# Cross-attention 0 of a four-part model: query weights folded into the keys, output weights into the values

## The reference, cut to what matters

```python
def _attn(x, ctx, Wq, Wk, Wv, Wo, bo):
    q = (x @ Wq).reshape(b, n, HEADS, DHEAD)
    k = (ctx @ Wk).reshape(b, m, HEADS, DHEAD)
    v = (ctx @ Wv).reshape(b, m, HEADS, DHEAD)
    scale = DHEAD ** (-0.5)
    sim = jnp.einsum('bihd,bjhd->bhij', q, k) * scale
    attn = jax.nn.softmax(sim, axis=-1)
    out = jnp.einsum('bhij,bjhd->bihd', attn, v).reshape(b, n, INNER)
    return out @ Wo + bo
...
h = _ln(x, g2, be2)
x = _attn(h, context, Wq2, Wk2, Wv2, Wo2, bo2) + x
```

## Time and profile before

| | us |
|---|---|
| median of 3 runs | 7044.72 |
| lowest, highest | 7041.6, 7048.59 |
| the profiled execution's own time | 7048.18 |
| its span (first to last instruction) | 7046.4 |

### The profile page before, as it was taken

The page is one execution under the profiler, slowest core; times in us unless marked ns, Lnnn a source line. Parts: engine busy times, 40 slices in busy tenths (PEclk is TensorE's granted clock), DMA queues, the critical chain, the costliest instruction groups (busy, mean ns, idle before and its releaser), DMA issues. The chain is left out here.

```text
span 7046.4 us, 74355 instructions
## 1 busy us (share of the span) xinstructions
PE 6239.0 (89%) x20890; PEld 2611.0 (37%) x20890; DVE 5161.7 (73%) x6021; ACT 3737.4 (53%) x6881; POOL 4712.8 (67%) x2193
## 2 busy tenths in 40 slices
PE   9999999999998888888888888888888888888898
PEld 4444445455343233322333222323222333223334
DVE  4444444454223999999999999999999999995623
ACT  4444444322223666666666666666666666664432
POOL 3333333211202999999999999999999999993300
PEclk9999999999999898999999998989898999999998
DMA  2000000100201232333323242323233333332000
GB/s 72 0 0 0 0 0 0 54 9 6 102 0 42 62 86 70 76 90 75 84 67 84 61 100 64 88 59 90 65 96 76 73 82 69 78 83 54 5 0 24
DMA packets 235646, 378.49 MB, mean 54 GB/s; under 512 B 62785, under 2 KB 71681, under 8 KB 233777
## 3 DMA queue, kind: packets, MB, share of 16 engines
q1 hardware_dynamic: 235312, 374.71, 21.9%
HBM read 202.29 MB, written 19.20 MB: 31 GB/s over the span
## 5 line engine op out<-in xcount | busy, mean ns | idle before, releaser
L2428 POOL TENSOR_TENSOR work<-work,weights 128x1024 f32<-128x1024 f32 x1152 | 2691.4, 2361 | 19.4 <-DMA weights<-mamba_bc 13.0
L2287 PE MATMUL banks<-work 128*64 128x512 f32 x4608 | 1371.2, 677 | 599.4 <-POOL work L2433 584.8
L2350 DVE TENSOR_TENSOR_SCAN banks<-banks,work 128x512 f32<-128x512 f32 x1296 | 1616.8, 1270 | 64.3 <-ACT banks L2397 64.3
L2397 ACT ACTIVATE banks<-work 128x512 f32<-128x512 f32 x2304 | 1497.7, 680 | 67.4 <-DVE work L2128 43.2
L2350 DVE TENSOR_TENSOR_SCAN work<-banks,work 128x512 f32<-128x512 f32 x1008 | 1264.4, 1269 | 102.1 <-ACT banks L2397 77.8
L2433 POOL TENSOR_TENSOR work<-work,weights 128x1024 f32<-128x1024 f32 x504 | 1187.4, 2356 | 92.3 <-ACT work L2020 92.3
L1860 PE MATMUL banks<-work,weights 128*128 128x512 f32 (+31 forms) x3796 | 1168.8, 459 | 3.0 <-DVE work L2101 3.0
L570 POOL TENSOR_TENSOR work<-work 128x1024 f32<-128x1024 f32 x256 | 484.0, 1893 | 801.6 <-DVE work L458 801.6
L1860 PEld LDWEIGHTS banks<-work,weights 128*128 128x128 f32 x3796 | 645.5, 193 | 625.2 <-issue 547.3
L2146 DVE TENSOR_TENSOR work<-banks,weights 128x512 f32<-128x512 f32 x1296 | 852.7, 669 | 0.0
L2287 PEld LDWEIGHTS banks<-work 128*64 128x64 f32 x4608 | 266.2, 144 | 1466.7 <-POOL work L2433 884.8
(11 more groups left out here) (297 smaller groups left out, 7641.0 us busy)
## 6 DMA issues: line engine op xcount, KB each, us to landing
weights<-mamba_bc SPq DMA_DIRECT2D x592, 256.0 KB, 5.0
work<-work SPq DMA_DIRECT2D x1160, 128.0 KB, 2.3
weights<-mamba_taps SPq DMA_DIRECT2D x5, 2048.0 KB, 7.3
mamba_taps<-work SPq DMA_DIRECT2D x4, 2048.0 KB, 6.9
work<-in_conv_rows SPq DMA_DIRECT2D x16, 256.0 KB, 6.7
out_T<-X SPq DMA_DIRECT2D x8, 512.0 KB, 3.3
X<-in_xT SPq DMA_DIRECT2D x2, 1536.0 KB, 13.0
weights<-in_in_w SPq DMA_DIRECT2D x5, 512.0 KB, 3.9
```

The lines of the kernel that those rows point to most:

```text
L2287: mm = e.matmul(ybank[k % 2][64 * h:64 * h + 64, :], fold, ring_pair(n, j)[:, h, :], start=False, stop=(a == SP_ - 1))
L2350: e.tensor_tensor_scan(ub if by_pool(j) else da, da, ub, state[:, i:i + 1], ALU.mult, ALU.add).then_inc(scanned, 1)
L2397: e.activation(banks[:, slot_of(i), :], dt_rep[:, k % 2, h, :], ACT.Exp, scale=decay[:, f:f + 1]).then_inc(da_full, 1)
L2428: e.tensor_tensor(ring_pair(n, j), u_rep[:, k % 2], bc[:, a, 0, :].unsqueeze(1).to_broadcast([P, 2, TC]), ALU.mult) \
```

## The change

cross_attention_0 is written anew. Keys are projected as before, values now with features on partitions. Then, for each head, the output weights are multiplied into the values (fold_values, 64 products over 64 partitions) and the query weights into the keys (fold_keys, 32 products over 64 partitions); heads alternate between partitions 0 to 63 and 64 to 127, and each of the pair writes a bank of its own. The folded keys (kq) stay in SBUF in four regions, some of them where weights lay. The folded values of all batches (8 MB) go to DRAM in four parts (lay) and come back one batch at a time (bring). Wq2 is passed in transposed. In the loop over tiles there is no query projection and no mixing: scores are 4 products of 512 columns over the normed features, and the output is 8 products for each of two halves straight from the transposed probabilities. The copy of a turned tile is one ScalarE operation on 1024 columns. The norm's scale is one GpSimd operation, its affine part stands behind the turned copy of tile t = 3.

VectorE's list and the set-up are left out here but for the regions:

```diff
+    folded, at = core.area(at, 3, 8, B * M)
+    keys, _ = core.area(2 * KD * T + KD * T + T, tiles, B * M)
+    values, _ = core.area(2 * KD * T + KD * T + T + QT * heads * M, tiles, B * M)
+    wq, wo = wview(core, side, 0, 8, D), wview(core, side, 6144, 8, D)
+    wk, wv = wview(core, side, 2048, 2, INNER), wview(core, side, 4096, 2, INNER)
+    wide = wview(core, side, 2048, 8, B * M)
+    kq = {(0, 0): folded[:, 0], (0, 1): folded[:, 1], (1, 0): folded[:, 2], (1, 1): wide}
+    REGIONS = ((0, 0), (0, 1), (1, 1), (1, 0))
+    staged = [core.weights[side][:, 2048:6144].rearrange("p (h e) -> p h e", h=heads),
+              folded[:, 2].rearrange("p h n -> p (h n)").rearrange("p (h e) -> p h e", h=heads),
+              wview(core, 0, 0, heads, D), wview(core, 0, 4096, heads, D)]
+    vo = [wview(core, side, 0, chunks, D), wview(core, side, 6144, chunks, D)]
...
+            def lay(p):
+                for half in range(2):
+                    for parity in range(2):
+                        e.wait_ge(copied[parity], (FOLDED_V + 8 * p + 4 * half + 4) // 2)
+                    e.dma_start(vo_dram[p][:, 8 * half:8 * half + 8, :], staged[p][:, 8 * half:8 * half + 8, :]).then_inc(laid[p], 16)
+
+            def bring(b):
+                for h in range(2):
+                    own = slice(width * h, width * h + width)
+                    src = vo_dram[b // 2][b % 2 * M:b % 2 * M + M, :, :].rearrange("m (c t) e -> m t c e", t=2)
+                    e.dma_start(vo[b % 2][own, :, :], src[:, h, :, :]).then_inc(vo_in[b % 2], 16)
+
+            for p in range(B // 2):
+                lay(p)
+            e.wait_ge(laid[0], 32)
+            e.wait_ge(copied[0], MADE // 2)
+            e.wait_ge(copied[1], MADE // 2)
+            bring(0)
+            bring(1)
+            e.wait_ge(laid[1], 32)
+            e.wait_ge(laid[2], 32)
+            e.wait_ge(laid[3], 32)
             load_weights(e, core, 0, [(0, d["L0_xattn_Wp"]), (4096, d["L0_xattn_W2"]), (6144, d["L1_xattn_pre_w1"]), (6656, d["L1_xattn_pre_w2"])])
             for b in range(2, B):
+                v_lane_read(e, ("out0", b - 2))
+                s_lane_read(e, ("out1", b - 2))
+                bring(b)
...
+            def bank_free(i):
+                if i >= RING_B:
+                    e.wait_ge(copied[i % 2], (i - RING_B) // 2 + 1)
+
+            def project_context(at):
+                for i in (at, at + 1):
+                    bank_free(i)
+                for k, r in enumerate(CROWS):
+                    for i in (at, at + 1):
+                        w, j = (wk, i) if i < VALUES else (wv, i - VALUES)
+                        mm = e.matmul(bank_of(i), w[0:r, k, j * P:(j + 1) * P], core.C[0:r, k, :], start=(k == 0), stop=(k == 1))
+                        if k == 1:
+                            mm.then_inc(made, 1)
+
+            def fold_values(at):
+                p, w = divmod(at - FOLDED_V, 8)
+                for i in (at, at + 1):
+                    bank_free(i)
+                for s in range(4):
+                    h, i = 2 * w + s, at + s % 2
+                    mm = e.matmul(bank_of(i)[:, s // 2 * D:s // 2 * D + D], values[rows_of(h), h // 2, p * P:(p + 1) * P], wo[rows_of(h), h // 2, :],
+                                  start=True, stop=True)
+                    if s >= 2:
+                        mm.then_inc(made, 1)
+
+            def fold_keys(at):
+                r, first = divmod(at - FOLDED_K, 8)
+                k, half = REGIONS[r]
+                for i in (at, at + 1):
+                    bank_free(i)
+                for s in range(2):
+                    h = 8 * half + first + s
+                    e.matmul(bank_of(at + s), wq[rows_of(h), h // 2, k * P:(k + 1) * P], keys[rows_of(h), h // 2, :], start=True, stop=True) \
+                        .then_inc(made, 1)
+
+            def project_out(b):
+                e.wait_ge(t_free, (b + 1) * QT)
+                e.wait_ge(vo_in[b % 2], 32 * (b // 2 + 1))
+                v_lane_free(e, ("out0", b))
+                for c in range(chunks):
+                    mm = e.matmul(lane_v, vo[b % 2][:, c, 0:P], probsT[:, c, :], start=(c == 0), stop=(c == chunks - 1))
+                mm.then_inc(ln.v_full, 1)
+                s_lane_free(e, ("out1", b))
+                for c in range(chunks):
+                    mm = e.matmul(lane_s, vo[b % 2][:, c, P:D], probsT[:, c, :], start=(c == 0), stop=(c == chunks - 1))
+                mm.then_inc(ln.s_full, 1)
+
+            def turn(n):
+                e.wait_ge(p_ready, n + 1)
+                e.wait_ge(t_free, n)
+                for c in range(chunks):
+                    mm = e.transpose(banks[:, 4 + c // 4, c % 4 * P:(c % 4 + 1) * P], probs[:, n % QT, c * P:(c + 1) * P], core.ident[:])
+                mm.then_inc(t_full, 1)
...
+            mean(0)
+            for i in range(0, FOLDED_V, 2):
+                project_context(i)
+                if i == 6:
+                    variance(0)
+            for p in range(2):
+                e.wait_ge(copied[p], FOLDED_V // 2)
+            for i in range(FOLDED_V, FOLDED_K, 2):
+                fold_values(i)
+            for i in range(FOLDED_K, MADE, 2):
+                fold_keys(i)
+            e.wait_ge(copied[0], MADE // 2)
+            e.wait_ge(copied[1], MADE // 2)
+            for n in range(TILES + BEHIND_T):
+                b, t = divmod(n, QT)
+                if n < TILES:
+                    if t == 0:
+                        e.wait_ge(nm.ready, b + 1)
+                    if n >= 2:
+                        e.wait_ge(shifted, n - 1)
+                    for half in range(2):
+                        for k in range(KD):
+                            mm = e.matmul(banks[:, 2 * (n % 2) + half, :], normed[:, b % 2, k, t * P:(t + 1) * P],
+                                          kq[k, half][:, :, b * M:(b + 1) * M], start=(k == 0), stop=(k == KD - 1))
                     mm.then_inc(s_full, 1)
+                if b + 1 < B and t == 0:
+                    mean(b + 1)
+                if b + 1 < B and t == 1:
+                    variance(b + 1)
+                if 1 <= b < B and t == 2:
+                    project_out(b - 1)
+                if n >= BEHIND_T:
+                    turn(n - BEHIND_T)
+            project_out(B - 1)
...
+            def affine(b):
+                e.wait_ge(nm.scaled, b + 1)
+                for k in range(KD):
+                    own = normed[:, b % 2, k, :]
+                    last = e.activation(own, own, ACT.Identity, scale=core.v("g2", k), bias=core.v("be2", k))
+                last.then_inc(nm.ready, 1)
...
+            for i in range(FOLDED_K + 1, MADE, 2):
+                room(e, i)
+                e.activation(destination(i), source(i), ACT.Copy, scale=width ** -0.5).then_inc(copied[1], 1)
+            for n in range(TILES + BEHIND_T):
+                b, t = divmod(n, QT)
+                if n < TILES:
+                    e.wait_ge(shifted, n + 1)
+                    e.activation(probs[:, t, :], probs[:, t, :], ACT.Exp).then_inc(exp_done, 1)
+                if b + 1 < B and t == 0:
+                    square(b + 1)
+                if b + 1 < B and t == 1:
+                    root(b + 1)
+                if n >= BEHIND_T:
+                    s = (n - BEHIND_T) % QT
+                    e.wait_ge(t_full, n - BEHIND_T + 1)
+                    e.activation(probsT[:, :, s * P:(s + 1) * P], banks[:, 4:6, :].rearrange("p a (c q) -> p (a c) q", c=4), ACT.Copy) \
+                        .then_inc(t_free, 1)
+                if b + 1 < B and t == 3:
+                    affine(b + 1)
...
+        "L0_xattn_Wq2": g("L0_xattn_Wq2").T,
     }
-    for n in ["L0_xattn_" + w for w in ("Wq1", "Wk1", "Wv1", "Wo1", "Wq2", "Wk2", "Wv2", "Wo2", "Wp", "W2")] + \
+    for n in ["L0_xattn_" + w for w in ("Wq1", "Wk1", "Wv1", "Wo1", "Wk2", "Wv2", "Wo2", "Wp", "W2")] + \
             ["L1_xattn_pre_w1", "L1_xattn_pre_w2"] + ["L2_xattn_" + w for w in ("Wq", "Wkv", "Wproj", "W1", "W2")]:
```

More of the change, by code:

```diff
@@ new lines, in v_lane_free, with v_lane_full, v_lane_read, s_lane_free @@
+    def v_lane_free(e, event):
+        e.wait_ge(ln.v_free, V[event])
+    def v_lane_full(e, event):
+        e.wait_ge(ln.v_full, V[event] + 1)
+    def v_lane_read(e, event):
+        e.wait_ge(ln.v_free, V[event] + 1)
+    def s_lane_free(e, event):
+        e.wait_ge(ln.s_free, S[event])
+    def s_lane_full(e, event):
+        e.wait_ge(ln.s_full, S[event] + 1)
+    def s_lane_read(e, event):
+        e.wait_ge(ln.s_free, S[event] + 1)
+    def destination(i):
+        if i < VALUES:
+            return keys[:, i, :]
+        if i < FOLDED_V:
+            return values[:, i - VALUES, :]
+        if i < FOLDED_K:
+            p, w = divmod(i - FOLDED_V, 8)
+            first = 4 * (w // 2) + w % 2
+            return staged[p][:, first:first + 3:2, :]
+        r, h = divmod(i - FOLDED_K, 8)
+        return kq[REGIONS[r]][:, h, :]
@@ L675, in _ @@
+            scale(0)
```

(46 more changed lines are left out.)

294 lines of the change are left out of this document (75 added, 219 removed).

## The result

| | us |
|---|---|
| changed kernel, median of 4 runs | 6995.59 (6988.93 to 6997.44) |
| kernel before beside it, median of 4 | 7044.8 (7041.6 to 7048.59) |
| ratio, 95% interval | 0.9925 (0.9913 to 0.9937) |
| profiled execution: time, span | 6994.55, 6992.4 |

The account below looks back on a forecast made before the run. TensorE was taken as the bound. Added 32.2 us, loop 326.8 us and slow-clock rows 16.4 us give 375.4 against 429.2 us, -54 us: 6990.5 us against the median, forecast range 6980 to 7002 at 0.55.

Parts of the forecast that it names:

- (a): Before the loop, 64 products folding output weights into the values: 15.0 us, or 27.5 us if row halves do not pair.
- (b): Before the loop, 32 products folding query weights into the keys: 15.4 us, or 27.5 us unpaired.
- affine, seven waits: In the loop, TensorE waits for the next batch's affine behind tile t = 3's copy: 5.6 us, seven times, 39.0 us.
- slow rows behind them: After each long TensorE wait the clock falls to 1.2 GHz and the next rows cost 2.06 us more.
- variance, six waits: In the loop, tile 1's variance waits for centring and square: 0.7 us six times, 4.2 us.
- end: waits and last residual: At the loop's end two turns wait on the softmax chain, then residual and signal: 9.8 us.
- The first rival: In the loop, the clock does not fall or the affine is not late: 6974 us, chance 0.14.
- Rival 2: In the folds, row halves do not pair: added 55.0 us instead of 30.4, so 7015 us, chance 0.10.
- (c) to (e): Around the folds: 64 evacuations hidden, two TensorE waits for copies 1.8 us together, 8 MB stored to DRAM at no cost.
- Rival 4: In the loop, scores over strided keys at double price: 110 us more, 7100 us, chance 0.07.
- Rival 3: In the loop, the softmax chain becomes the bound, 2 to 3 us a batch more: 7010 us, chance 0.10.
- Rival 5: Whole change: the fold saves nothing, products and waits cancel within 0.2%, chance 0.04.

Follow-up runs that it names:

- Run 1: Changed kernel with the next batch's affine moved behind the Exp of tile t = 2 in ScalarE's list: 6957.16 us, ratio 0.9868 to the kernel before.
- Run 2: Changed kernel with five unused 512-column products added on TensorE before each affine wait of batches 1 to 7: 6979.14 us, ratio 0.9901 to the kernel before.
- run 3: Changed kernel with the key fold's heads reordered 0, 2, 4, 6, 1, 3, 5, 7, so one half's stand together: 6999.83 us, ratio 0.993 to before.
- run 4: Changed kernel with every product of the value fold made twice into the same place: 7005.7 us, ratio 0.994 to the kernel before.
- run 6: The change's folds in the batch order of the kernel before, four score tiles, output projection, then four turns: 6935.07 us, ratio 0.9842 to before.

## Why the prediction was right, step by step

The stage's change was forecast as -54 us and measured as -54.16. The terms, from the rows above:

| term | forecast, us | measured, us |
|---|---|---|
| (a) value fold | 15.0 | 14.25 |
| (b) key fold | 15.4 | 13.8 |
| added before the loop in all | 32.2 | 30.5 |
| loop's work on TensorE | 271.8 | taken as 271.8: tiles of 3.43 |
| affine, seven waits | 39.0 | 6 x 5.34 + 4.39 = 36.4 |
| slow rows behind them | 14.4 | 15.6 |
| variance, six waits | 4.2 | 6 x 0.51 = 3.1 |
| batch 0, two turns | 2.0 | 1.8 |
| turn 27, in batch 7 | 0 | 1.9 |
| end: waits and last residual | 9.8 | 8.9 |
| end: slow rows | 2.06 | 4.4 |
| loop and tail in all | 343.2 | 344.6 |

The first three rows: before the first fold the stage takes 34.80 us and took 33.22, so 1.6 of the 30.5 us lie there, where the forecast had put one seam only; the two seams measured 0.73 and 0.75. Waits are counted here from the end of the rows' issue to the next start, as in the forecast (1479.33 + 0.88 to 1485.55 is 5.34; the view's own figure, 5.18, counts from the modelled end). The loop is 1375.05 to 1718.88 + 0.75, the end of the last residual:

```profile
1718.88 0.75 DVE L841 SCALAR_TENSOR_TENSOR X<-banks,vec,X 128x512 f32<-128x512 f32 x1 [6.12 <-PE banks L781]
```

What the table leaves over is 0.7 us. The loop's work on TensorE is not a measurement: it is the forecast's own sum, and the measured rows beside it have its price.

- **The affine wait** was the step on which the forecast rested, and it was right in mechanism and size: 5.34 against 5.6. Run 1 shows the cause by taking it away.
- **The clock.** Right on the mean, too simple in form. Each wait was followed by slow rows, but they cost 2.9 and 1.8 us in turn (6.28 and 5.18 us for a tile's eight rows and not 3.43); the single row taken from the second cross-attention, 2.06, lay between. At the end the slow rows ran on through two turns and into the output projection: 4.4 us and not 2.06. Run 2 shows by itself that this is the clock. The first rival, that it wouldn't fall, is out.
- **Pairing of row halves.** Rival 2 is out: both folds ran at the paired price (0.11 and 0.215 us a row), and run 3 shows that part of it hangs on the order.
- **Covered copies and DMAs, (c) to (e).** No wait inside the folds but the two seams, 0.73 and 0.75 us; run 4 shows the copies covered. The 16 loads of folded values landed in 6.8 us (median) and no TensorE wait names them.
- **Strided keys.** Rival 4 is out. A tile's eight score rows take 1453.82 + 0.86 - 1451.24 = 3.44 us, 0.43 each, the price of contiguous rows. The Trainium skill (SBUF — State Buffer, Door 1: The DMA port swizzle) says that consecutive accesses to the same 16-byte line run at full bandwidth; taken as in the forecast, runs of 256 bytes should then be free, and the trace agrees.
- **Softmax chain as the bound.** Rival 3 is out for the steady batches: in run 6 the same chain fits behind 34.4 us of TensorE work a batch. Rival 5, that nothing is saved, is out by the 49 to 54 us.
- **What was missed** is small: turn 27 waits 1.9 us in the last batch, where no mean and variance products stand before it any more; waits fell 1.1 short for the variance and 2.6 for the affine. These misses cancelled, and so did 1.7 us of folds that were cheaper against the slow rows at the end. That the stage came out within 0.2 us of the forecast is luck; single terms were off by up to 2.6 us.
- **What the forecast didn't say** is that its 39 + 14 us of affine wait and clock weren't the price of the folds, but of where one step stands. It named them as the largest loss and went no further; runs 1 and 6 are the answer.

## What to carry to other kernels

When a loop form is copied from another place, look in each engine's list for the step of the next iteration that the copied form puts behind this iteration's work, and ask what TensorE has left to do until it is there: here one misplaced affine gave back 40 of 113 us. A wait of 5 us on TensorE was followed by slow rows here, some 2 us of them, and is to be priced with them. Where the wait can't go, filling it gave those 2 us back even with useless work (run 2); that useful work would give its own duration besides is an expectation that no run here tests. Before taking over a new order, cost the same algebra in the old one: the plain order, whose long output projection covers the whole chain in steady batches, had the shortest stage here (349.83 and 347.26 us) and the lowest times (6933 to 6935 us).

## What the runs showed of the hardware

- After a wait of 5.2 us the clock was at its lower level of 1.2 GHz for the next rows each time, but not for equally long: six score rows took 5.49, 4.49, 5.49, 4.50, 5.49 and 4.51 us in successive batches, with the same wait of 5.18 before each. Ten rows whose results were thrown away kept it at 2.4 GHz, although a wait of 0.88 remained.
- Rows that followed each other alone ran 0.429 us apart, and rows on the two halves of TensorE's partitions ran beside each other, in two chains: strict alternation gave 64 rows in 13.93 us, groups by half 18.76.
- Products that read their moving operand as eight runs of 64 f32, 512 apart, had the price of contiguous ones, 0.43 us for 512 columns.
- The last stage of the program, with the same instructions, took 84.6 us in one execution and 77.6 in another, at granted clocks of 0.69 and 0.74; a difference of two spans holds such movements, a difference of one stage's lengths doesn't.
